# Attention with its quarters in pairs: another order of scores, raw tiles and weighted values on TensorE

## The chip, the cores and the metric

The kernel runs on one core of a Trainium2 chip. The metric is the device time of one execution in microseconds; the figure for a kernel is the median of several executions. Engines work in order, each through its own queue, and meet through semaphores: TensorE (PE, with its weight loads as PEld), VectorE (DVE), ScalarE (ACT), GpSimd (POOL) and SyncE (SP), which here only issues DMAs.

## What is computed

One block of a network on an input of 4 images of 32 x 32 tokens with 192 channels: a layer norm, attention with a decomposed relative position bias, a residual, a second layer norm, and a mixture of 8 experts of which each token takes one. Only the attention matters here:

```python
B, H, W, DIM, HEADS = (4, 32, 32, 192, 12)
HD = DIM // HEADS                       # 16
n = h * w                               # 1024 tokens
q, k, v = (qkv[0], qkv[1], qkv[2])      # (b * heads, n, hd)
rel_h = jnp.einsum('bhwc,hkc->bhwk', r_q, Rh)
rel_w = jnp.einsum('bhwc,wkc->bhwk', r_q, Rw)
bias = (rel_h[:, :, :, :, None] + rel_w[:, :, :, None, :]).reshape(b * heads, n, n)
attn = jax.nn.softmax(jnp.einsum('bnd,bmd->bnm', q * scale, k) + bias, axis=-1)
out = jnp.einsum('bnm,bmd->bnd', attn, v)
```

That is 4 x 12 = 48 maps of 1024 x 1024. The text calls each of the 48 a head and numbers them 0 to 47.

## The kernel before, in words

The stages run one after the other: projections with the relative terms (to about 138 us), the attention (to about 672 us), gate, routing and experts. Only the attention's function differs in the change.

**What a head needs.** The softmax subtracts a row maximum, which is found first. For a head, TensorE makes eight raw tiles (raw_scores, L750, matmuls at L759): 128 queries by 1024 keys, in one of two PSUM buffers (max_ps, two banks each). VectorE reduces each one to its negated maximum (take_max, L900, the reduce at L905). GpSimd repeats the maxima (L657), TensorE transposes them (transpose_max, L782, into a score bank), ScalarE copies them (copy_max, L865) and SyncE stores them as one more row of the queries' side (store_max). Only then are the scores proper made (scores, L787, matmul at L791): sixteen matmuls of 128 keys by 512 queries, k = 0 to 15, each into one of three PSUM banks (ring_ps). ScalarE takes the exponential of each (L888) into one of eight tiles of probs. weighted_values (L795, matmuls at L803) multiplies four of them with the values and adds into out_ps; a program line of eight matmuls there is sixteen in the trace, since the operands are four bytes wide. When all sixteen are in, ScalarE copies out_ps (copy_out, L872), TensorE turns it (turn_out, L809, matmuls at L812, into a score bank), and VectorE divides by the sums (normalize, L907 to L920, which ends with att_sb).

**The order.** A head is four quarters, u = 0 to 3. In each, TensorE issues scores 4u and 4u+1, a pair of raw tiles, scores 4u+2 and 4u+3, and weighted_values of the quarter before. The raw tiles are the last two of head n+1 in quarter 0, and the first six of head n+2 in quarters 1 to 3. Quarter 1 ends with transpose_max for head n+1, quarter 2 with turn_out for head n-1. VectorE's order is two reduces a quarter, and normalize of head n-1 behind those of quarter 2. ScalarE's is four exps a quarter, the output copy behind exp 3, and the copy of the maxima behind exp 7.

**The waits that the prediction uses.** A raw tile waits until the tile two before it is reduced (tile_max, L755), because its buffer is the same. The three score banks go around in turns; eighteen turns a head: sixteen scores, one turn for the transposed maxima (MAX_AT, turn 8) and one for the turned output (TURNED_AT, turn 13). bank_free (L763) finds what stood in the bank three turns before, and waits for its exp (exp_done), for the copy of the maxima (max_copied) or for normalize (att_done). With turn 13, the score at turn 16, k = 14, is the one that waits for att_done; scores 9 and 10 come at turns 10 and 11.

**Ends of the stage.** The heads run in groups of four; the first and the last group are written out, those between are a loop. Head 0 has no output of a head before; head 46 has raw tiles in quarter 0 alone and head 47 has none.

Of the kernel before, what the change touches and what calls it, by code (L numbers as in the profile page):

```python
# [552 lines left out]
def attention(nc, g):  # L553
# [7 lines left out]
    GROUP = 4  # L561
    RING = 2 * GROUP
    BANKS = 3
    MAX_AT, TURNED_AT, TURN = 8, 13, 2 * KT + 2
    HIGH = HD + 2 * HS
    with ExitStack() as ctx:
        sb = lambda name, shape, dt=F32: ctx.enter_context(nc.sbuf_tensor(name, shape, dt))
# [37 lines left out]
        def slot(s, ahead=0):  # L605

            return (s.slot + ahead) % SLOTS

        def head(s, ahead=0):


            return s.group + (s.slot + ahead) // SLOTS
# [132 lines left out]
        @block.tensor  # L745
        def _(pe):
            pe.wait_ge(consts_loaded, 16 * 2 * SLOTS)
            pe.wait_ge(ident_cast, 1)

            def raw_scores(n, j, t, reused):  # L750


                if reused:

                    pe.wait_ge(tile_max, KT * n + t - 1)  # L755
                for quarter in (0, 2, 1, 3):
                    at = quarter // 2 * LOWER
                    keys = slice(quarter * QN, (quarter + 1) * QN)
                    last = nc.tensor.matmul(max_ps[t % 2][:, keys], q_side[j][at:at + HIGH, quarter, t * P:(t + 1) * P],  # L759
                                            k_side[j][at:at + HIGH, keys], start=True, stop=True, skip_group_check=True, tile_position=(at, 0))  # L760
                last.then_inc(raw_ready, 1)

            def bank_free(s, at):  # L763

                at, back = at - BANKS, 0
                while True:
                    if at < 0:
                        at, back = at + TURN, 1  # L770
                        if not s.before(1):
                            return
                    if at == MAX_AT and (back or s.after(1)):
                        return pe.wait_ge(max_copied, s.n - back + 2)
                    if at == TURNED_AT and s.before(1 + back):
                        return pe.wait_ge(att_done, s.n - back)
                    if at not in (MAX_AT, TURNED_AT):
                        k = at - (at > MAX_AT) - (at > TURNED_AT)
                        return pe.wait_ge(exp_done, 2 * KT * (s.n - back) + k + 1)
                    at -= BANKS  # L780

            def transpose_max(n, j):  # L782
                pe.wait_ge(max_repeated, n + 1)
                nc.tensor.matmul(max_t_ps, max_copies[:, j % 2, :, :].rearrange("p q t -> p (q t)"), ident16[:],
                                 start=True, stop=True).then_inc(max_t_ready, 1)

            def scores(s, u, i):  # L787

                k, tile = GROUP * u + i, 2 * u + i // 2
                bank_free(s, turn_of(k))  # L790
                nc.tensor.matmul(ring_ps[turn_of(k) % BANKS][:], k_side[slot(s)][:, tile * P:(tile + 1) * P],  # L791
                                 q_side[slot(s)][:, tile // 2, (i % 2) * HALF:(i % 2 + 1) * HALF],
                                 start=True, stop=True).then_inc(scores_ready, 1)

            def weighted_values(n, j, u):  # L795


                pe.wait_ge(exp_done, 2 * KT * n + GROUP * u + GROUP)
                for i in range(2):
                    tile = 2 * u + i  # L800
                    for quarter in range(QUARTERS):
                        queries = slice(quarter % 2 * QN, (quarter % 2 + 1) * QN)
                        last = nc.tensor.matmul(out_ps[quarter * 2 * HD:(quarter + 1) * 2 * HD, :], values[j][:, tile, :],  # L803
                                                probs[:, u % 2 * GROUP + 2 * i + quarter // 2, queries],
                                                start=(tile == 0), stop=(tile == KT - 1), skip_group_check=True,
                                                tile_position=(0, quarter * 2 * HD))
                last.then_inc(group_done, 1)

            def turn_out(n):  # L809
                pe.wait_ge(out_copied, n + 1)  # L810
                for b in range(2):
                    last = nc.tensor.transpose(turned_ps[:, b * P:(b + 1) * P], out_t[:, b * P:(b + 1) * P], g.ident[:])  # L812
                last.then_inc(turned, 1)


            for n, tiles in ((0, KT), (1, 6)):
                pe.wait_ge(loaded[n], 16 * LOADS)
                for t in range(tiles):
                    raw_scores(n, n, t, KT * n + t >= 2)
                if n == 0:  # L820
                    transpose_max(0, 0)

            def step(s):
                for u in range(PAIR_TILES):
                    if u == 0:

                        pe.wait_ge(max_loaded[slot(s)], 16 * (head(s) + 1))
                    if u == 1 and s.after(2):
                        pe.wait_ge(loaded[slot(s, 2)], 16 * LOADS * (head(s, 2) + 1))
                    scores(s, u, 0)  # L830
                    scores(s, u, 1)
                    for i in range(2):

                        if u == 0 and s.after(1):
                            raw_scores(s.n + 1, slot(s, 1), 6 + i, True)
                        if u >= 1 and s.after(2):
                            raw_scores(s.n + 2, slot(s, 2), 2 * (u - 1) + i, True)
                    scores(s, u, 2)
                    scores(s, u, 3)
                    if u == 0 and s.before(1):  # L840
                        weighted_values(s.n - 1, slot(s, -1), PAIR_TILES - 1)
                    if u == 1:
                        pe.wait_ge(values_ready, s.n + 1)
                        if s.before(1):

                            pe.wait_ge(out_copied, s.n)
                    if u >= 1:
                        weighted_values(s.n, slot(s), u - 1)
                    if u == 1 and s.after(1):
                        bank_free(s, MAX_AT)  # L850
                        transpose_max(s.n + 1, slot(s, 1))
                    if u == 2 and s.before(1):
                        bank_free(s, TURNED_AT)
                        turn_out(s.n - 1)

            steps(pe, BH, SLOTS, step)
            weighted_values(BH - 1, (BH - 1) % SLOTS, PAIR_TILES - 1)
            pe.wait_ge(exp_done, 2 * KT * BH)
            turn_out(BH - 1)

        @block.scalar
        def _(act):
            nc.scalar.activation(ident16[:], g.ident[:], ACT.Copy).then_inc(ident_cast, 1)  # L863

            def copy_max(n, j, fills):  # L865
                act.wait_ge(max_t_ready, n + 1)
                if fills is not None:

                    act.wait_ge(max_loaded[(j - 2) % SLOTS], 16 * fills)
                nc.scalar.activation(max_rows[:, j % 2, :], max_t_ps, ACT.Copy).then_inc(max_copied, 1)  # L870

            def copy_out(n, reused):  # L872
                act.wait_ge(group_done, PAIR_TILES * (n + 1))
                if reused:
                    act.wait_ge(turned, n)
                nc.scalar.activation(out_t[:], out_ps[:], ACT.Copy).then_inc(out_copied, 1)

            copy_max(0, 0, None)

            def step(s):  # L880
                for u in range(PAIR_TILES):
                    for i in range(GROUP):
                        k = GROUP * u + i
                        if i == 0 and (s.before(1) or u >= 2):

                            act.wait_ge(group_done, PAIR_TILES * s.n + u - 1)
                        act.wait_ge(scores_ready, 2 * KT * s.n + k + 1)
                        nc.scalar.activation(probs[:, u % 2 * GROUP + i, :], ring_ps[turn_of(k) % BANKS][:], ACT.Exp).then_inc(exp_done, 1)  # L888
                        if u == 0 and i == 3 and s.before(1):
                            copy_out(s.n - 1, s.before(2))  # L890
                        if k + 1 == MAX_AT and s.after(1):

                            copy_max(s.n + 1, slot(s, 1), head(s, -1) + 1 if s.before(1) else None)

            steps(act, BH, SLOTS, step)
            copy_out(BH - 1, True)

# [787 lines left out]
```

## Time and profile before

| | us |
|---|---|
| median of three executions | 913.78 (912.25 to 915.0) |
| profiled execution | 914.5 |
| its span in the trace | 912.5 |
| attention, first to last output copy | 163.0 to 671.0 |
| PE, DVE, ACT busy over the span | 825.7, 726.4, 605.2 |

The profile is of one execution. PE counts as busy while a matmul is under way, and matmuls overlap; so a busy PE is not yet PE at its limit. Starts of neighbouring groups say more than their durations. In a timeline, a line is a run of like instructions: start, duration of the run, engine, line of the program, output and inputs, shapes, count. What stands in brackets is the idle time of the engine ahead of it, and who ended it.

### The profile page before, as it was taken

The numbers are of one execution on the slowest core, as the hardware profiler recorded it, in microseconds if no ns is written. First come the engines' busy times: TensorE is split into PE (matmuls) and PEld (weight loads), VectorE is DVE, ScalarE is ACT, GpSimd is POOL, SyncE is SP. The second block draws the span as 40 slices with busy tenths as digits, with TensorE's granted clock in tenths as the row PEclk, the third lists the DMA queues.
The fourth block names the chain that finished last, engine by engine and source line by source line (L and its number), as shares of the span: only waits on it lengthen the run. The fifth ranks groups of instructions, "written<-read, shape, count | busy, mean of one in ns | idle before, by whom it ended". The sixth has DMA issues, their size and how long they took to land. (4 is left out here: it accounts for less than half of the span.)

```text
span 912.5 us, 26072 instructions
## 1 busy us (share of the span) xinstructions
PE 825.7 (90%) x8906; PEld 465.2 (51%) x8906; DVE 726.4 (80%) x1019; ACT 605.2 (66%) x1140; POOL 274.8 (30%) x430
## 2 busy tenths in 40 slices
PE   3889937999999999999999999999979936999994
PEld 1657922333333333333333333333359926999994
DVE  6765867998989989999999989989527676888883
ACT  3555624888888888888888888888854403545452
POOL 3360000013343343302224342421114403555552
PEclk9899965999999999999999999999989757999997
DMA  6234883344554545444454444553034402222220
GB/s 170 78 102 123 347 287 93 99 120 130 141 132 116 128 131 140 116 115 131 116 139 133 131 130 134 143 141 102 7 146 138 156 24 61 84 84 78 89 61 11
DMA packets 69700, 109.60 MB, mean 120 GB/s; under 512 B 20107, under 2 KB 36649, under 8 KB 68114
## 3 DMA queue, kind: packets, MB, share of 16 engines
q1 hardware_dynamic: 59120, 75.49, 29.6%
q0 software_dynamic: 9216, 26.51, 10.0%
q10 hardware_dynamic: 1314, 6.95, 2.0%
q8 instruction: 30, 0.49, 0.2%
q14 instruction: 20, 0.16, 0.1%
HBM read 77.58 MB, written 33.19 MB: 121 GB/s over the span
## 5 line engine op out<-in xcount | busy, mean ns | idle before, releaser
L905 DVE TENSOR_REDUCE neg_max<-max_ps 128x1 f16<-128x1024 f32 x384 | 452.3, 1222 | 54.8 <-PE max_ps L759 54.4
L888 ACT ACTIVATE probs<-ring_ps 128x512 f32<-128x512 f32 x768 | 413.7, 595 | 69.7 <-PE ring_ps L791 68.3
L791 PE MATMUL ring_ps<-q_side,k_side 113*128 113x512 f16 x768 | 234.4, 387 | 6.5 <-DMA q_side<-rel_split 4.4
L803 PE MATMUL out_ps<-probs,values 128*32 128x256 f32 x3072 | 206.4, 386 | 0.1
L759 PE MATMUL max_ps<-k_side,q_side 48*128 48x256 f16 x1536 | 122.7, 279 | 16.0 <-ACT ident L863 9.6
L803 PEld LDWEIGHTS out_ps<-probs,values 128*32 128x32 f32 x3072 | 80.3, 109 | 111.1 <-ACT probs L888 56.5
L657 POOL COPY max_copies<-neg_max 128x32 f16<-128x32 f16 x48 | 10.1, 210 | 366.1 <-DVE neg_max L905 366.1
L759 PEld LDWEIGHTS max_ps<-k_side,q_side 48*128 48x128 f16 x1536 | 50.1, 95 | 114.7 <-issue 66.8
L791 PEld LDWEIGHTS ring_ps<-q_side,k_side 113*128 113x128 f16 x768 | 51.8, 97 | 105.4 <-ACT probs L888 74.1
L1438 PE MATMUL hid_ps<-slot_t,w_top 128*118 128x128 f16 x312 | 69.7, 223 | 0.8 <-ACT slot_t L1484 0.8
L1441 PE MATMUL hid_ps<-slot_t,w_tail 128*118 128x128 f16 x312 | 69.1, 221 | 0.0
L1440 PE MATMUL hid_ps<-slot_t,w_top 128*118 128x128 f16 x312 | 69.1, 221 | 0.0
L1439 PE MATMUL hid_ps<-slot_t,w_top 128*118 128x128 f16 x312 | 69.0, 221 | 0.0
L1442 PE MATMUL hid_ps<-slot_t,w_tail 128*118 128x128 f16 x312 | 69.0, 221 | 0.0
L1494 ACT ACTIVATE silu<-hid_ps 118x512 f32<-118x512 f32 x39 | 23.3, 597 | 50.1 <-PE hid_ps L1442 50.1
L1417 POOL DMA_INDIRECT out<-y,slot_token x39 | 39.6, 1014 | 54.8 <-issue 38.0
L1402 POOL DMA_INDIRECT slot_rows<-token_rows,slot_token x39 | 41.7, 1070 | 37.7 <-SPq L1365 26.1
L1541 DVE TENSOR_TENSOR hidden<-hid_ps,silu 118x512 f32<-118x512 f32 x39 | 27.0, 692 | 25.7 <-ACT silu L1494 18.2
L1438 PEld LDWEIGHTS hid_ps<-slot_t,w_top 128*118 128x118 f16 x312 | 42.0, 134 | 3.6 <-issue 1.3
L1442 PEld LDWEIGHTS hid_ps<-slot_t,w_tail 128*118 128x118 f16 x312 | 42.1, 135 | 0.0
L1439 PEld LDWEIGHTS hid_ps<-slot_t,w_top 128*118 128x118 f16 x312 | 42.1, 135 | 0.0
L1441 PEld LDWEIGHTS hid_ps<-slot_t,w_tail 128*118 128x118 f16 x312 | 42.1, 135 | 0.0
(216 smaller groups left out, 1339.2 us busy)
## 6 DMA issues: line engine op xcount, KB each, us to landing
q_side<-rel_split SPq DMA_DIRECT2D x384, 64.0 KB, 2.3
q_side<-qk_split SPq DMA_DIRECT2D x192, 64.0 KB, 2.5
rel_split<-expert_weights ACTq DMA_DIRECT2D x6, 1024.0 KB, 4.9
rel_split<-expert_weights SPq DMA_DIRECT2D x6, 1024.0 KB, 5.7
q_side<-qk_split SPq DMA_DIRECT2D x48, 128.0 KB, 2.8
k_side<-qk_split SPq DMA_DIRECT2D x144, 32.0 KB, 1.8
token_rows<-tn_parts SPq DMA_DIRECT2D x8, 512.0 KB, 2.9
expert_weights<-in_w_t POOLq DMA_DIRECT2D x32, 117.2 KB, 2.9
```

Source lines behind the costliest of these rows:

```text
L759: last = nc.tensor.matmul(max_ps[t % 2][:, keys], q_side[j][at:at + HIGH, quarter, t * P:(t + 1) * P], k_side[j][at:at + HIGH, keys], star ...
L791: nc.tensor.matmul(ring_ps[turn_of(k) % BANKS][:], k_side[slot(s)][:, tile * P:(tile + 1) * P], q_side[slot(s)][:, tile // 2, (i % 2) * HA ...
L803: last = nc.tensor.matmul(out_ps[quarter * 2 * HD:(quarter + 1) * 2 * HD, :], values[j][:, tile, :], probs[:, u % 2 * GROUP + 2 * i + quar ...
L888: nc.scalar.activation(probs[:, u % 2 * GROUP + i, :], ring_ps[turn_of(k) % BANKS][:], ACT.Exp).then_inc(exp_done, 1)
L905: nc.vector.tensor_reduce(neg_max[:, j % 2, t:t + 1], max_ps[t % 2][:], AX, ALU.max, negate=True).then_inc(tile_max, 1)
L1402: pool.indirect_dma_start(rows[:, j, :], None, g.token_rows, bass.IndirectOffsetOnAxis(ap=g.slot_token[:, n:n + 1], axis=0), bounds_check= ...
L1417: pool.indirect_dma_start(g.out_rows, bass.IndirectOffsetOnAxis(ap=g.slot_token[:, n:n + 1], axis=0), y[:, j, :], None, bounds_check=last_ ...
L1438: nc.tensor.matmul(out, w_top[:, j, h, 0, some], hi_top, start=True, stop=False, skip_group_check=True)
L1439: nc.tensor.matmul(out, w_top[:, j, h, 0, some], lo_top, start=False, stop=False, skip_group_check=True)
L1440: nc.tensor.matmul(out, w_top[:, j, h, 1, some], hi_top, start=False, stop=False, skip_group_check=True)
L1441: nc.tensor.matmul(out, w_tail[:, j, h, some], hi_tail, start=False, stop=False, skip_group_check=True)
L1442: last = nc.tensor.matmul(out, w_tail[:, j, h, some], lo_tail, start=False, stop=True, skip_group_check=True)
```

## The change

The four quarters are written as two pairs. In a pair (quarters u and u+1) TensorE now issues: scores 4u, 4u+1 and 4u+2; the raw pair of quarter u; weighted_values of the quarter before; three scores (4u+3, 4u+4, 4u+5); the raw pair of quarter u+1; scores 4u+6 and 4u+7; weighted_values of quarter u. turn_out moves from the end of quarter 2 to behind the weighted values in the middle, ahead of score 11, and with it the turn of its bank from 13 to 12. transpose_max stays behind the weighted values of quarter 0. On ScalarE the output copy goes ahead of exp 3 instead of behind it. The wait for the loads of head n+2 stands directly ahead of the raw pair of quarter 1. All counts stay the same.

```diff
-    MAX_AT, TURNED_AT, TURN = 8, 13, 2 * KT + 2
+    MAX_AT, TURNED_AT, TURN = 8, 12, 2 * KT + 2
...
             def step(s):
-                for u in range(PAIR_TILES):
+                pe.wait_ge(max_loaded[slot(s)], 16 * (head(s) + 1))
+                for u in range(0, PAIR_TILES, 2):
+                    for i in range(3):
+                        scores(s, u, i)
+                    raw_pair(s, u)
+                    if u:
+                        weighted_values(s.n, slot(s), u - 1)
+                    elif s.before(1):
+                        weighted_values(s.n - 1, slot(s, -1), PAIR_TILES - 1)
+                    if u and s.before(1):
+                        bank_free(s, TURNED_AT)
+                        turn_out(s.n - 1)
+                    scores(s, u, 3)
+                    scores(s, u + 1, 0)
+                    scores(s, u + 1, 1)
+                    if u == 0 and s.after(2):
+                        pe.wait_ge(loaded[slot(s, 2)], 16 * LOADS * (head(s, 2) + 1))
+                    raw_pair(s, u + 1)
+                    scores(s, u + 1, 2)
+                    scores(s, u + 1, 3)
...
+                    weighted_values(s.n, slot(s), u)
...
+                        if k == 3 and s.before(1):
+                            copy_out(s.n - 1, s.before(2))
                         act.wait_ge(scores_ready, 2 * KT * s.n + k + 1)
...
-                        if u == 0 and i == 3 and s.before(1):
-                            copy_out(s.n - 1, s.before(2))
```

raw_pair(s, u) issues the two raw tiles that belong to quarter u, as the loop did before.

TensorE in quarters 0 and 1 of head 2, before (q_side2 and k_side2 are this head's operands; max_ps0 and max_ps1 are the raw tiles, of heads 3 and then 4, whose operands lie in slot 0):

```order
L791 MATMUL ring_ps0<-q_side2,k_side2 128x512
L791 MATMUL ring_ps1<-q_side2,k_side2 128x512
L759 MATMUL max_ps0<-k_side3,q_side3 128x256 x4
L759 MATMUL max_ps1<-k_side3,q_side3 128x256 x4
L791 MATMUL ring_ps2<-q_side2,k_side2 128x512
L791 MATMUL ring_ps0<-q_side2,k_side2 128x512
L803 MATMUL out_ps<-probs,values1 32x256 x8
L791 MATMUL ring_ps1<-q_side2,k_side2 128x512
L791 MATMUL ring_ps2<-q_side2,k_side2 128x512
L759 MATMUL max_ps0<-k_side0,q_side0 128x256 x4
L759 MATMUL max_ps1<-k_side0,q_side0 128x256 x4
```

And of the change, the same place:

```order
L791 MATMUL ring_ps0<-q_side2,k_side2 128x512
L791 MATMUL ring_ps1<-q_side2,k_side2 128x512
L791 MATMUL ring_ps2<-q_side2,k_side2 128x512
L759 MATMUL max_ps0<-k_side3,q_side3 128x256 x4
L759 MATMUL max_ps1<-k_side3,q_side3 128x256 x4
L803 MATMUL out_ps<-probs,values1 32x256 x8
L791 MATMUL ring_ps0<-q_side2,k_side2 128x512
L791 MATMUL ring_ps1<-q_side2,k_side2 128x512
L791 MATMUL ring_ps2<-q_side2,k_side2 128x512
L759 MATMUL max_ps0<-k_side0,q_side0 128x256 x4
L759 MATMUL max_ps1<-k_side0,q_side0 128x256 x4
```

Between the two raw pairs there were two scores, the weighted values and two scores; now there are the weighted values and three scores.

TensorE in quarters 2 and 3 of head 2, before, from turn_out on, with the semaphores that each one waits for (raw tiles of head 4, in slot 0):

```order
L812 MATMUL ring_ps1<-ident_sb,out_t 128x128 [waits out_copied,exp_done]
L812 MATMUL ring_ps1<-ident_sb,out_t 128x128
L791 MATMUL ring_ps2<-q_side2,k_side2 128x512 [waits exp_done]
L791 MATMUL ring_ps0<-q_side2,k_side2 128x512 [waits exp_done]
L759 MATMUL max_ps0<-k_side0,q_side0 128x256 [waits tile_max]
L759 MATMUL max_ps0<-k_side0,q_side0 128x256 x3
L759 MATMUL max_ps1<-k_side0,q_side0 128x256 [waits tile_max]
L759 MATMUL max_ps1<-k_side0,q_side0 128x256 x3
L791 MATMUL ring_ps1<-q_side2,k_side2 128x512 [waits att_done]
L791 MATMUL ring_ps2<-q_side2,k_side2 128x512 [waits exp_done]
```

And of the change:

```order
L812 MATMUL ring_ps0<-ident_sb,out_t 128x128 [waits out_copied,exp_done]
L812 MATMUL ring_ps0<-ident_sb,out_t 128x128
L791 MATMUL ring_ps1<-q_side2,k_side2 128x512 [waits exp_done]
L791 MATMUL ring_ps2<-q_side2,k_side2 128x512 [waits exp_done]
L791 MATMUL ring_ps0<-q_side2,k_side2 128x512 [waits att_done]
L759 MATMUL max_ps0<-k_side0,q_side0 128x256 [waits tile_max]
L759 MATMUL max_ps0<-k_side0,q_side0 128x256 x3
L759 MATMUL max_ps1<-k_side0,q_side0 128x256 [waits tile_max]
L759 MATMUL max_ps1<-k_side0,q_side0 128x256 x3
L791 MATMUL ring_ps1<-q_side2,k_side2 128x512 [waits exp_done]
L791 MATMUL ring_ps2<-q_side2,k_side2 128x512 [waits exp_done]
```

The score that waits for att_done is now k = 13 and stands ahead of the raw pair of quarter 3; before it was k = 14, behind that pair.

## Rows read from the trace of the kernel before

**Rows 1.** Windows: length, busy PE, PEld, DVE, ACT, POOL, clock, DMA share, GB/s.
```profile
200.00:640.00 440.00, 437.36 (x4658) 163.00 (x4653) 397.08 (x407) 372.06 (x729) 132.42 (x235) 1.00 0.48 128
...
660.00:670.00 10.00, 8.78 (x85) 3.16 (x87) 0.50 (x2) 8.61 (x17) 0.00 (x0) 1.00 0.01 2
670.00:680.00 10.00, 5.88 (x40) 4.75 (x34) 2.38 (x5) 4.02 (x7) 2.34 (x1) 0.70 0.60 229
```

**Rows 2.** Timeline of TensorE's matmuls over one head in mid stage.
```profile
399.87 0.60 PE L791 MATMUL ring_ps<-q_side,k_side 113*128 113x512 f16 x2
400.40 0.62 PE L759 MATMUL max_ps<-k_side,q_side 48*128 48x256 f16 x8
...
401.50 1.07 PE L803 MATMUL out_ps<-probs,values 128*32 128x256 f32 x16
402.50 0.61 PE L791 MATMUL ring_ps<-q_side,k_side 113*128 113x512 f16 x2
403.04 0.61 PE L759 MATMUL max_ps<-k_side,q_side 48*128 48x256 f16 x8
403.58 0.60 PE L791 MATMUL ring_ps<-q_side,k_side 113*128 113x512 f16 x2
404.12 1.07 PE L803 MATMUL out_ps<-probs,values 128*32 128x256 f32 x16
405.00 0.22 PE L784 MATMUL ring_ps<-ident,max_copies 128*32 128x128 f16 x1
405.15 0.60 PE L791 MATMUL ring_ps<-q_side,k_side 113*128 113x512 f16 x2
405.69 0.61 PE L759 MATMUL max_ps<-k_side,q_side 48*128 48x256 f16 x8
...
406.77 1.07 PE L803 MATMUL out_ps<-probs,values 128*32 128x256 f32 x16
...
408.05 0.60 PE L791 MATMUL ring_ps<-q_side,k_side 113*128 113x512 f16 x2
408.58 0.61 PE L759 MATMUL max_ps<-k_side,q_side 48*128 48x256 f16 x8
409.12 0.61 PE L791 MATMUL ring_ps<-q_side,k_side 113*128 113x512 f16 x2
409.66 1.07 PE L803 MATMUL out_ps<-probs,values 128*32 128x256 f32 x16
410.66 0.39 PE L791 MATMUL ring_ps<-q_side,k_side 113*128 113x512 f16 x1
```

**Rows 3.** The line of the output copy: count, durations in ns, first and last start.
```profile
L876 ACT ACTIVATE out_t<-out_ps x48: 383/383/384, 163.0 to 671.0; 128x256 f32<-128x256 f32 x48
```

**Rows 4.** Timeline of VectorE over the same head.
```profile
403.47 2.36 DVE L905 TENSOR_REDUCE neg_max<-max_ps 128x1 f16<-128x1024 f32 x2 [0.27 <-PE max_ps L759]
406.13 2.36 DVE L905 TENSOR_REDUCE neg_max<-max_ps 128x1 f16<-128x1024 f32 x2 [0.30 <-PE max_ps L759]
...
408.74 0.29 DVE L920 TENSOR_TENSOR att_sb<-ring_ps,recip 128x128 f32 x1
```

**Rows 5.** TensorE's timeline from 403.5 on: the second raw tile of that pair.
```profile
403.27 0.38 PE L759 MATMUL max_ps<-k_side,q_side 48*128 48x256 f16 x4
```

**Rows 6.** Waits from 200 to 640 us: total, times, longest.
```profile
PEld ring_ps L791 <- DVE att_sb L920: 8.7, 41, 0.2
```

**Rows 7.** Timeline of ScalarE in the same head.
```profile
402.63 0.38 ACT L876 ACTIVATE out_t<-out_ps 128x256 f32<-128x256 f32 x1 [0.16 <-PE out_ps L803]
402.93 2.17 ACT L888 ACTIVATE probs<-ring_ps 128x512 f32<-128x512 f32 x4
405.29 0.27 ACT L870 ACTIVATE max_rows<-ring_ps 32x128 f16<-32x128 f32 x1 [0.20 <-PE ring_ps L784]
```

**Rows 8.** TensorE's timeline in head 0, where the granted clock was at its lower level.
```profile
149.90 1.03 PE L791 MATMUL ring_ps<-q_side,k_side 113*128 113x512 f16 x2 [1.91 <-DMA q_side<-rel_split]
150.87 1.03 PE L759 MATMUL max_ps<-k_side,q_side 48*128 48x256 f16 x8
```

## What I predicted before the changed kernel had run

> **What bounds the kernel now.** I read the windows of the attention stage first. From 200 to 640 us TensorE shows as busy in all but 2.6 of 440 us at full clock, while VectorE is busy for 397 us of it [rows 1]. "Busy" only says that matmuls overlap, so the next view is TensorE's timeline over one head (one of the 48 attention maps) [rows 2]. The starts give the price of each piece, gap to the next included. Two scores followed by raw tiles take 0.54 us (402.50 to 403.04); one more score in such a group adds 0.22 (0.61 less the 0.39 of one). The raw pair followed by scores takes 0.54, two scores followed by weighted values 0.54, weighted values followed by scores 1.00 (409.66 to 410.66), or 1.03 with the maxima's transpose behind them (404.12 to 405.15), or 1.28 with turn_out (406.77 to 408.05). A plain quarter is 0.54 + 0.54 + 0.54 + 1.00 = 2.62 and a head is 10.79 (399.87 to 410.66). Over all heads the output copies, 48 of them from 163.0 to 671.0, give 508 / 47 = 10.81 [rows 3].
>
> So far TensorE looks like the bound. VectorE's timeline tells the rest [rows 4]. The first raw tile of a pair at 403.04 lets its reduce start at 403.47 (0.43 later). The two reduces take 2.36 and end at 405.83. The second raw tile of a pair may not start before the second reduce of the pair before has emptied its PSUM buffer: those reduces began 0.44 behind the raw tiles of 400.40 (as 405.69 to 406.13) and ended at about 403.20, and the second raw tile starts at 403.27 [rows 5]. First raw tile to second raw tile of the next pair is therefore 403.27 - 400.40 = 2.87 us at least. In the order before, the natural distance is 2.62 + 0.23 = 2.85, so this **second loop, TensorE to VectorE and back, is as tight as TensorE's own order**. VectorE idles 0.27 to 0.30 a quarter, not because it has time but because both raw tiles of a pair come together.
>
> There is one more loop in each head. In quarter 2 turn_out writes the previous head's turned output into a score bank. normalize reads it, standing in VectorE's queue behind the two reduces of that quarter: it ends at 409.03 (408.74 + 0.29) [rows 4]. The score that reuses the bank is then the first behind raw pair 3, at 409.12. The waits show 41 of these, 8.7 us in all, 0.21 each [rows 6], the size of the gap that stands between pieces anyway. It is nearly free, because the raw pair of quarter 3 had gone out at 408.58, ahead of it.
>
> **The change part by part.** *Fewer switches on TensorE.* Two quarters had eight groups: four of scores (4 x 0.54), two raw, two of weighted values. Now there are seven: 0.76 + 0.76 + 0.54 = 2.06 for the scores instead of 2.16, so 0.10 less in two quarters. Raw tiles followed directly by weighted values do not occur in the trace. Bounds: nothing for the switch, so 0.46 for the two raw tiles (two steps of 0.23, 403.04 to 403.27), and at the dear end 0.46 + 0.28, the dearest insertion that the rows show (turn_out with its two matmuls, 1.28 less 1.00). I take 0.54, the nearest rows being raw to scores. Below it turns out not to matter.
>
> *Raw pairs at uneven distance.* Call the start of a raw pair zero. Inside a pair of quarters the order is raw, weighted values, three scores, raw: 0.54 + 1.00 + 0.76 = 2.30 to the next pair, and 2.53 to its second tile. It may not start before 2.87 [rows 5]. TensorE stands for 0.34 us in front of its own queue: two scores and weighted values are behind it. Between pairs of quarters the way is longer, and VectorE idles there. The unknown switch could cost 0.34 more or any amount less and the second tile would still come at 2.87.
>
> *The bank of turn_out moves from ring turn 13 to 12.* This is the expensive part. The turned output now lies in bank 0, and the score that comes three turns later is the thirteenth counted from zero. It stands **ahead of** raw pair 3, where in the old order the waiting score was behind it. Normalize is still queued behind the reduces of raw pair 2. TensorE would reach that score 0.54 + 1.28 + 0.44 = 2.26 after raw pair 2; it may go at 409.12 - 405.69 = 3.43 (raw pair 2 to the score that waits for normalize, as measured [rows 2, 4]). That is 1.17 us of stall. Behind it stand raw pair 3 and everything after; VectorE, done with normalize, has no raw tile and idles as well, so nothing is won back later.
>
> *The output copy on ScalarE goes ahead of exp 3.* It starts 1.13 behind the weighted values (401.50 to 402.63) [rows 2, 7], so 1.67 after raw pair 0, and frees ScalarE at 2.05; exp 3 would have begun at 0.54 + 1.00 + 0.43 = 1.97. It costs exp 3 0.08. With 0.54 an exp (2.17 for four) exp 7 ends at 4.77, while the copy of the maxima starts at 3.72 + 0.88 + 0.29 = 4.89 and ends at 5.16; score 10, which uses that bank, is due at 5.19. Margin nil: I give it 0 to 0.1 a head and take 0. The wait for loaded moves a few tenths of a microsecond later and costs nothing. SyncE's and GpSimd's orders don't change.
>
> *The sum.* The path that now closes one head: raw pair 2 to score 13, 3.43; score 13 to raw pair 3, 0.32; raw pair 3, 0.54; scores 14 and 15, 0.54; weighted values, 1.00; three scores of the next head, 0.76; raw pair 0 to second tile of raw pair 1, 2.87; that tile to score 6, 0.31 (403.27 to 403.58); scores 6 and 7, 0.54; weighted values with transpose, 1.03; scores 8 to 10, 0.76. Together **12.10 us against 10.79, 1.31 more a head**. It holds for heads 1 to 45, which have both raw pairs and a normalize: 45 x 1.31 = 59.0. Head 0 has no normalize, only uneven pairs, at low clock: 0 to 1, I take 0.5. Heads 46 and 47 have hardly any raw tiles: 0. Sum 59.5 on the profiled execution's own 914.5 us gives 974.0; the median before is 0.7 below that execution, so about **973 us**, 6.5% slower.
>
> **The rivals.** *A: the switches decide.* If neither loop held TensorE back, 0.10 less twice a head would be 48 x 0.2 = 9.6 us: 904. The Trainium skill (TensorEngine Tiling, Key Properties) says that changing the tiling mode drains the engine, and one drain fewer in eight is what this order has. The rows agree that a switch costs about 0.1 us, but a gain needs the raw tiles to find VectorE ready, and 2.87 against 2.53 speaks against it. It would need the second reduce to end over 0.3 us sooner. 4%.
>
> *B: normalize doesn't hold score 13,* and only the uneven pairs count. Then raw pair 2 to the second tile of pair 3 is 2.87 too; normalize (about 0.54) and two reduces then end at 5.70, so the next second tile comes at 5.77, and the half takes 5.77 - 0.23 = 5.54; the other half 2.87 + 0.31 + 0.54 + 1.03 + 0.76 = 5.51. 11.05 a head: 45 x 0.26 + 0.5 = 12 more, 926. Against it: VectorE works in order, and the old trace shows normalize ending just where the reduces let it. 6%.
>
> *C: the stalls bring TensorE's clock down.* TensorE would stand 1.5 of 12.1 us a head, the longest time 1.2. From 660 to 670 us it was idle for 1.2 of 10 us and kept 1.00; the clock fell only where it was idle for 4 of 10 (670 to 680) [rows 1]. At the low clock two scores before raw tiles take 0.97 instead of 0.54 [rows 8], 1.8 times; the 5.8 us of TensorE's own pieces on the path would grow by 4.6 a head. A quarter of the heads gives 11 x 4.6 = 51 more: 1024. The Trainium skill (TensorE: Matmul & The Clock Gate, "A second HAM failure mode: psum-queue depth-cycling") tells of a kernel whose short idles between groups made the clock swing; no row here shows that. 4%.
>
> **How the numbers follow.** The forecast's mechanism has 84%, A 4, B 6, C 4, something else 2. Within it: the path's eleven pieces are read to 0.01 and could be 0.1 short; the ScalarE margin adds up to 0.1 a head, a bank of the third score in a row as much: up to 9 us more, 983. Downwards the mean head may hide a part of the new stalls in its irregular waits (10.81 against 10.79 leaves little) and score 13 might come 0.2 sooner: 45 x 0.25 = 11 less, 962. The range is 962 to 984, leaving out the rivals. A measurement of this kernel can tell about 0.3% from no change. Faster by more has 4%, within it 1%, slower 95%.
>
> **What would show it.** Heads of about 12.1 us; a wait of scores for att_sb of 1.1 to 1.3 us once a head, about 55 us in all against 8.7 in the waits; a wait of the raw tiles for neg_max of about 0.5 once a head; VectorE idling before neg_max about 2 us a head; clock at 1.00. Wrong would be a head under 11.3 with no long wait for att_sb (A or B) or a clock below 1.00 (C).

## The result, and the profile after

The changed kernel took 967.2 us in the median (964.74 to 969.46) against 914.39 for the kernel before (912.25 to 915.24). The median before is now over four executions, where the table above had three. The ratio on record is 1.0589, with a 95% interval of 1.0556 to 1.0621; the two medians divided give 1.0578, inside it. The forecast was 973 with a range of 962 to 984. The profiled execution took 964.74, its span in the trace is 962.7.

TensorE's timeline over one head, as [rows 2] for the kernel before (start, duration of the run, engine, line, operation, names, shapes, count; in brackets the idle time ahead and who ended it):

```profile
406.97 0.61 PE L759 MATMUL max_ps<-k_side,q_side 48*128 48x256 f16 x8
407.51 1.07 PE L803 MATMUL out_ps<-probs,values 128*32 128x256 f32 x16
408.51 0.44 PE L812 MATMUL ring_ps<-ident_sb,out_t 128*128 128x128 f32 x2
408.78 0.60 PE L791 MATMUL ring_ps<-q_side,k_side 113*128 113x512 f16 x2
410.36 0.39 PE L791 MATMUL ring_ps<-q_side,k_side 113*128 113x512 f16 x1 [0.98 <-DVE att_sb L926]
410.68 0.61 PE L759 MATMUL max_ps<-k_side,q_side 48*128 48x256 f16 x8
411.23 0.61 PE L791 MATMUL ring_ps<-q_side,k_side 113*128 113x512 f16 x2
411.76 1.07 PE L803 MATMUL out_ps<-probs,values 128*32 128x256 f32 x16
412.76 0.82 PE L791 MATMUL ring_ps<-q_side,k_side 113*128 113x512 f16 x3
413.52 0.61 PE L759 MATMUL max_ps<-k_side,q_side 48*128 48x256 f16 x8
414.06 1.07 PE L803 MATMUL out_ps<-probs,values 128*32 128x256 f32 x16
415.06 0.82 PE L791 MATMUL ring_ps<-q_side,k_side 113*128 113x512 f16 x3
415.82 0.39 PE L759 MATMUL max_ps<-k_side,q_side 48*128 48x256 f16 x4
416.37 0.39 PE L759 MATMUL max_ps<-k_side,q_side 48*128 48x256 f16 x4 [0.16 <-DVE neg_max L911]
416.69 0.61 PE L791 MATMUL ring_ps<-q_side,k_side 113*128 113x512 f16 x2
417.23 1.07 PE L803 MATMUL out_ps<-probs,values 128*32 128x256 f32 x16
...
418.27 0.84 PE L791 MATMUL ring_ps<-q_side,k_side 113*128 113x512 f16 x3
419.04 0.61 PE L759 MATMUL max_ps<-k_side,q_side 48*128 48x256 f16 x8
```

From raw pair 2 to raw pair 2 is 419.04 - 406.97 = 12.07 us. Both stalls stand in it. Score 13 (410.36) comes 3.39 after raw pair 2, and raw pair 3 behind it. Scores 11 and 12 take 0.44 where a score follows them directly, so score 13 would have started at 408.78 + 0.44 = 409.22; it stands for 1.14. The raw pair at 415.82 is torn apart: its second tile is at 416.37, 0.55 later instead of 0.23, and 2.85 behind the pair of 413.52.

VectorE over the same stretch, as [rows 4]:

```profile
407.40 2.36 DVE L911 TENSOR_REDUCE neg_max<-max_ps 128x1 f16<-128x1024 f32 x2 [0.95 <-PE max_ps L759]
409.67 0.20 DVE L921 RECIPROCAL recip<-ring_ps 128x8 f32<-128x8 f32 x1
410.01 0.29 DVE L926 TENSOR_TENSOR att_sb<-ring_ps,recip 128x128 f32 x1
411.12 2.36 DVE L911 TENSOR_REDUCE neg_max<-max_ps 128x1 f16<-128x1024 f32 x2 [0.81 <-PE max_ps L759]
413.95 4.66 DVE L911 TENSOR_REDUCE neg_max<-max_ps 128x1 f16<-128x1024 f32 x4 [0.48 <-PE max_ps L759]
```

Normalize ends at 410.30 and score 13 starts 0.06 later. From there VectorE has nothing to reduce until 411.12. The four reduces from 413.95 on run without a gap: there TensorE waits for VectorE. In the three places in brackets VectorE waits for TensorE, 0.48 to 0.95 us at a time, where before it was 0.27 to 0.30.

The waits from 200 to 640 us (total, times, longest), as [rows 6]; the two queues of TensorE, weight loads and matmuls, record the same stall apart:

```profile
DVE neg_max L911 <- PE max_ps L759: 80.3, 109, 1.0
PEld ring_ps L791 <- DVE att_sb L926: 53.3, 36, 1.5
...
PE ring_ps L791 <- DVE att_sb L926: 35.6, 36, 1.0
PEld max_ps L759 <- DVE neg_max L911: 31.0, 72, 0.4
```

The wait for att_sb is 53.3 / 36 = 1.48 us a head on the weight loads, against 8.7 / 41 = 0.21 in [rows 6]. This record counts the usual 0.2 between groups and the loading ahead as well, so it is more than the stall of 1.14. The windows and the line of the output copy, as [rows 1, 3]:

```profile
200.00:640.00 440.00, 398.34 (x4171) 153.84 (x4169) 354.29 (x363) 330.00 (x653) 123.25 (x216) 1.00 0.41 116
```

```profile
L882 ACT ACTIVATE out_t<-out_ps x48: 384/384/402, 160.9 to 724.4; 128x256 f32<-128x256 f32 x48
```

TensorE is idle for 41.7 of 440 us and its clock stays at 1.00. First to last output copy takes 563.5 us against 508.0.

### The profile page after: what moved, and what is told of

It is laid out like the page before. It is cut to its first block and busy times, and to the rows that moved or that the text cites. A ratio compares the mean times of both kernels' runs of the same rounds, so it can differ in the third digit from the quotient of the medians.

```text
span 962.7 us, 26072 instructions
## 1 busy us (share of the span) xinstructions
PE 828.8 (86%) x8906; PEld 470.4 (49%) x8906; DVE 723.2 (75%) x1019; ACT 601.2 (62%) x1140; POOL 276.1 (29%) x430
## 5 line engine op out<-in xcount | busy, mean ns | idle before, releaser
L791 PE MATMUL ring_ps<-q_side,k_side 113*128 113x512 f16 x768 | 228.6, 386 | 45.3 <-DVE att_sb L926 44.3
L759 PE MATMUL max_ps<-k_side,q_side 48*128 48x256 f16 x1536 | 129.9, 279 | 23.6 <-DVE neg_max L911 13.4
L791 PEld LDWEIGHTS ring_ps<-q_side,k_side 113*128 113x128 f16 x768 | 55.8, 97 | 173.5 <-DVE att_sb L926 67.3
L803 PEld LDWEIGHTS out_ps<-probs,values 128*32 128x32 f32 x3072 | 80.3, 109 | 94.7 <-ACT probs L896 30.8
L759 PEld LDWEIGHTS max_ps<-k_side,q_side 48*128 48x128 f16 x1536 | 55.7, 95 | 106.8 <-DVE neg_max L911 51.4
L1444 PEld LDWEIGHTS hid_ps<-slot_t,w_top 128*118 128x118 f16 x312 | 41.8, 134 | 4.1 <-issue 1.8
L1445 PEld LDWEIGHTS hid_ps<-slot_t,w_top 128*118 128x118 f16 x312 | 42.0, 134 | 0.0
L1446 PEld LDWEIGHTS hid_ps<-slot_t,w_top 128*118 128x118 f16 x312 | 42.0, 134 | 0.0
L1447 PEld LDWEIGHTS hid_ps<-slot_t,w_tail 128*118 128x118 f16 x312 | 41.9, 134 | 0.0
```

What stands on the lines that cost most here:

```text
L1444: nc.tensor.matmul(out, w_top[:, j, h, 0, some], hi_top, start=True, stop=False, skip_group_check=True)
L1445: nc.tensor.matmul(out, w_top[:, j, h, 0, some], lo_top, start=False, stop=False, skip_group_check=True)
L1446: nc.tensor.matmul(out, w_top[:, j, h, 1, some], hi_top, start=False, stop=False, skip_group_check=True)
L1447: nc.tensor.matmul(out, w_tail[:, j, h, some], hi_tail, start=False, stop=False, skip_group_check=True)
```

## The experiments

Each kernel ran beside the kernel before on the same chip; ratios are to that kernel's time there (median 912.13 us for the first four, 912.45 for the three with half reduces). "A head" is the mean distance of output copies over the first 44 of the 47 intervals, the ends of the stage left out. For the kernel before it is 10.87 us, for the changed one 12.11. The kernel before has eight long intervals, 10.93 to 11.73, which raise its mean; its middle interval (the median of the 44) is 10.80.

**The bank of turn_out moved back.** The changed order, with turn_out one score later:

```diff
-    MAX_AT, TURNED_AT, TURN = 8, 12, 2 * KT + 2
+    MAX_AT, TURNED_AT, TURN = 8, 13, 2 * KT + 2
...
+                    scores(s, u, 3)
                     if u and s.before(1):
                         bank_free(s, TURNED_AT)
                         turn_out(s.n - 1)
-                    scores(s, u, 3)
```

> The changed kernel with one thing undone: turn_out goes behind score 11 instead of ahead of it, its bank gets turn 13 again, so that score 14, behind raw pair 3, is the one that waits for normalize. Theory (normalize holds score 13 ahead of raw pair 3): the wait of scores for att_sb falls from 1.5 to about 0.2 us a head. Not all of it comes back: score 13 now uses score 11's bank and waits for its exp (turn_out between them), about 0.4. Head 11.2 us, time about 930 (924 to 938). If instead the time of the change comes from the uneven raw pairs, or from the new order as such, the kernel stays at 955 or more.

Measured: 930.39 us, ratio 1.0211 (1.0171 to 1.0251), 11.34 a head. TensorE in quarters 2 and 3:

```profile
404.46 0.61 PE L759 MATMUL max_ps<-k_side,q_side 48*128 48x256 f16 x8
405.00 1.07 PE L803 MATMUL out_ps<-probs,values 128*32 128x256 f32 x16
406.00 0.39 PE L791 MATMUL ring_ps<-q_side,k_side 113*128 113x512 f16 x1
406.23 0.38 PE L812 MATMUL ring_ps<-ident_sb,out_t 128*128 128x128 f32 x2
406.45 0.38 PE L791 MATMUL ring_ps<-q_side,k_side 113*128 113x512 f16 x1
407.08 0.39 PE L791 MATMUL ring_ps<-q_side,k_side 113*128 113x512 f16 x1 [0.25 <-ACT probs L896]
407.40 0.61 PE L759 MATMUL max_ps<-k_side,q_side 48*128 48x256 f16 x8
```

Raw pair 2 to raw pair 3 is 2.94 us instead of 3.71. Moving turn_out one score later, its bank with it, is worth 0.77 us a head. The wait for att_sb falls to 0.21 a head, as expected:

```profile
PEld ring_ps L791 <- DVE att_sb L926: 8.2, 39, 0.2
```

Not all comes back: score 13 now waits for the exp of score 11, as expected, and starts 0.63 behind score 12 instead of 0.22.

**The same bank in the old order.** The kernel before, with turn_out between scores 10 and 11:

```diff
-    MAX_AT, TURNED_AT, TURN = 8, 13, 2 * KT + 2
+    MAX_AT, TURNED_AT, TURN = 8, 12, 2 * KT + 2
...
                     scores(s, u, 2)
+                    if u == 2 and s.before(1):
+                        bank_free(s, TURNED_AT)
+                        turn_out(s.n - 1)
                     scores(s, u, 3)
...
-                    if u == 2 and s.before(1):
-                        bank_free(s, TURNED_AT)
-                        turn_out(s.n - 1)
```

> The order of the kernel before, with only turn_out moved: between scores 10 and 11, bank at turn 12. Raw pairs stay evenly spaced. Score 13, ahead of raw pair 3, waits for normalize. Theory: that wait alone makes the head 11.6 us (raw pair 2 to score 13 is 3.43 as before, raw pair 3 follows 0.32 later, 3.75 instead of 2.88), time about 948 (940 to 956). Rival (the pairs' uneven distance is the cost, the bank is not): within 5 us of 914.

Measured: 945.68 us, ratio 1.0381 (1.0347 to 1.0415), 11.62 a head. The raw pairs stand evenly in the issue order here, and the kernel still loses nearly two thirds of what the change loses. TensorE, from the score ahead of the waiting one:

```profile
401.46 0.39 PE L791 MATMUL ring_ps<-q_side,k_side 113*128 113x512 f16 x1
402.51 0.39 PE L791 MATMUL ring_ps<-q_side,k_side 113*128 113x512 f16 x1 [0.65 <-DVE att_sb L920]
402.83 0.61 PE L759 MATMUL max_ps<-k_side,q_side 48*128 48x256 f16 x8
```

So the order of the groups isn't needed for this part. That a score waits for normalize ahead of raw pair 3 is enough.

**The new order in quarters 0 and 1 only.** The loop over pairs of quarters runs for u = 0; quarters 2 and 3 and the bank of turn_out are as before; ScalarE's order is the changed one:

```diff
-    MAX_AT, TURNED_AT, TURN = 8, 12, 2 * KT + 2
+    MAX_AT, TURNED_AT, TURN = 8, 13, 2 * KT + 2
...
+                for u in range(2, PAIR_TILES):
+                    scores(s, u, 0)
+                    scores(s, u, 1)
+                    raw_pair(s, u)
+                    scores(s, u, 2)
+                    scores(s, u, 3)
+                    weighted_values(s.n, slot(s), u - 1)
+                    if u == 2 and s.before(1):
+                        bank_free(s, TURNED_AT)
+                        turn_out(s.n - 1)
```

> Quarters 0 and 1 in the new order (with the new place of the output copy on ScalarE), quarters 2 and 3 and turn_out with its bank at turn 13 in the old one. This leaves the uneven raw pairs and one switch fewer. Theory: the second tile of raw pair 1 waits 0.3 to 0.4 us a head for neg_max; the head is 10.95 to 11.05 us, the first head shorter by 2 as in the change; time 916 to 924. Rival A (a saved switch is a gain): 910 or less.

Measured: 917.32 us, ratio 1.0063 (1.0042 to 1.0084), 11.01 a head, 0.14 more than the mean before and 0.21 more than its middle interval. The torn pair shows:

```profile
404.20 0.82 PE L791 MATMUL ring_ps<-q_side,k_side 113*128 113x512 f16 x3
404.95 0.39 PE L759 MATMUL max_ps<-k_side,q_side 48*128 48x256 f16 x4
405.50 0.39 PE L759 MATMUL max_ps<-k_side,q_side 48*128 48x256 f16 x4 [0.16 <-DVE neg_max L913]
```

The uneven distance costs, but little: the smaller of the two mechanisms. The second tile stands for 0.32 (405.50 less 404.95 less 0.23), the saved switch gives 0.10 back, and 0.22 is left, which is the 0.21 of the middle interval.

The two costs taken alone don't add up to the change: 0.75 and 0.14 are 0.89 of 1.25 a head. The rest shows in the timelines. In the kernel before, the raw pairs start at 405.69, 408.58 and, a quarter on, at

```profile
411.20 0.62 PE L759 MATMUL max_ps<-k_side,q_side 48*128 48x256 f16 x8
```

Raw pair 2 to raw pair 3 grows from 2.89 to 3.71, raw pair 3 to the next raw pair 0 from 2.62 to 2.84, and from there to the next raw pair 2 from 5.29 (400.40 to 405.69) to 5.52. In the new order one score fewer and one switch fewer stand ahead of score 13. TensorE arrives there sooner and only waits longer, 1.14 us against 0.83 in the old order (402.51 less 401.46 less 0.22), while the score that moved takes its time behind raw pair 3.

**The output copy back behind exp 3.** The changed kernel with ScalarE's old order:

```diff
-                        if k == 3 and s.before(1):
-                            copy_out(s.n - 1, s.before(2))
...
+                        if k == 3 and s.before(1):
+                            copy_out(s.n - 1, s.before(2))
```

> The changed kernel with the output copy on ScalarE back behind exp 3. Exp 3 cannot start before score 3, which now stands behind the weighted values, so the copy, ready before that, comes 0.4 to 0.9 later and with it exps 4 to 7 and the copy of the maxima. Theory: that is 0.2 us a head on the path through scores 6 to 10, time 976 (970 to 982). Rival (ScalarE has slack everywhere): unchanged at 967.

Measured: 965.39 us, ratio 1.0595 (1.0565 to 1.0625), the interval of the change itself, and 12.11 a head, the same. My expectation was wrong. ScalarE in this kernel:

```profile
402.52 0.60 ACT L894 ACTIVATE probs<-ring_ps 128x512 f32<-128x512 f32 x1 [0.72 <-PE ring_ps L791]
403.02 0.38 ACT L882 ACTIVATE out_t<-out_ps 128x256 f32<-128x256 f32 x1
403.28 2.08 ACT L894 ACTIVATE probs<-ring_ps 128x512 f32<-128x512 f32 x4
405.52 0.27 ACT L876 ACTIVATE max_rows<-ring_ps 32x128 f16<-32x128 f32 x1 [0.16 <-PE ring_ps L784]
```

and in the changed kernel:

```profile
403.04 0.38 ACT L882 ACTIVATE out_t<-out_ps 128x256 f32<-128x256 f32 x1 [0.43 <-PE out_ps L803]
403.33 2.71 ACT L896 ACTIVATE probs<-ring_ps 128x512 f32<-128x512 f32 x5
406.32 0.27 ACT L876 ACTIVATE max_rows<-ring_ps 32x128 f16<-32x128 f32 x1 [0.28 <-PE ring_ps L784]
```

Counted from score 3 (402.10 here, 402.90 there), the output copy starts 0.78 later (0.92 instead of 0.14), but exp 3 starts 0.42 behind the score here and 0.43 there: the copy ahead of it only fills a time in which ScalarE waits for score 3. Exp 7 ends at 3.26 instead of 3.14, so 0.12 later and not 0.4 to 0.9. The copy of the maxima waits for its transpose in both of these heads; from 200 to 640 us this wait is recorded 37 times in the changed kernel and 18 times here, so the margin is used up in about half of the heads. The place of this copy costs nothing that the time shows.

**Half reduces.** In three kernels each reduce reads 512 of the 1024 keys, so that the maximum over the other half is left out; this shortens VectorE's two reduces from 2.36 to 1.29 us and changes nothing in any order:

```diff
-                nc.vector.tensor_reduce(neg_max[:, j % 2, t:t + 1], max_ps[t % 2][:], AX, ALU.max, negate=True).then_inc(tile_max, 1)
+                nc.vector.tensor_reduce(neg_max[:, j % 2, t:t + 1], max_ps[t % 2][:, 0:HALF], AX, ALU.max, negate=True).then_inc(tile_max, 1)
```

On the kernel before:

> The kernel before, but each reduce reads 512 of its 1024 keys (the maximum over the other half is left out), so that VectorE's part of the loop falls from 2.36 to about 1.3 us a pair. Theory: TensorE's own order was nearly as tight as the loop, so little comes back: 10.6 a head instead of 10.8, 0.2 x 47 = 9 us less, about 903 to 908. If VectorE had been the bound, 40 us or more would come back.

Measured: 906.68 us, ratio 0.9941 (0.9920 to 0.9962), 10.79 a head. VectorE loses over 45% of its reduce time and the kernel 0.6%. TensorE's own order was the other bound, hardly looser. The time fell where I expected it, the head didn't: I had written 10.6. The middle interval hardly moved, 10.78 against 10.80; most of the 0.08 is that seven of the eight long intervals are gone.

On the changed kernel:

> The changed kernel with the same half reduces. Theory: both VectorE's parts of the loss shrink, the second raw tile of raw pair 1 no longer waits, and the wait of score 13 for normalize falls to the time from turn_out on, about 0.5 us instead of 1.3; 11.1 a head, about 1.0 less than the changed kernel: 920 to 930. Rival (the new order itself costs TensorE its time, whatever VectorE does): 955 or more.

Measured: 924.06 us, ratio 1.0116 (1.0089 to 1.0144), 11.19 a head. Of the change's 5.9% only 1.2% is left, or 1.9% above the half-reduce kernel in the old order. The wait for normalize is still there, shorter (0.30 us of idle time on the matmuls instead of 0.98), and now it comes from turn_out and no longer from the reduces: VectorE itself waits for the turned output.

```profile
402.34 0.39 PE L791 MATMUL ring_ps<-q_side,k_side 113*128 113x512 f16 x1 [0.30 <-DVE att_sb L926]
```

```profile
400.05 1.29 DVE L911 TENSOR_REDUCE neg_max<-max_ps 128x1 f16<-128x512 f32 x2 [1.66 <-PE max_ps L759]
401.64 0.21 DVE L921 RECIPROCAL recip<-ring_ps 128x8 f32<-128x8 f32 x1 [0.29 <-PE ring_ps L812]
```

On the kernel with the new order in quarters 0 and 1 only:

> New order in quarters 0 and 1 only, old order and turn 13 in quarters 2 and 3, with half reduces. Nothing of VectorE is in the way now, so the saved switch (0.1 us a head, 5 us) should show against x5_old_half_reduce if rival A's arithmetic holds on TensorE. My working says that ScalarE takes it back: exp 3 waits behind the output copy, scores 7 and 9 then wait 0.1 each for their banks' exps, 10.66 against 10.58 a head. Expected: 0 to 4 us above x5; rival A: 4 to 6 below it.

Measured: 900.94 us, ratio 0.9876 (0.9851 to 0.9901), 10.74 a head. That is 5.7 us below the old order with half reduces, with intervals that don't touch, and rival A's arithmetic rather than mine. With full reduces the same order lost 0.6%. Whether a group less pays thus depends on VectorE. This kernel also has ScalarE's new order and the later wait for the loads, which no run takes apart here. The timeline doesn't settle why it pays so much: the second raw tile no longer waits, but scores 6 and 7 take 0.65 us (409.32 to 409.97) in the head below and 0.58 in the one before it, instead of 0.54, because score 7 waits for an exp as my working had it. That eats the saved 0.1 wholly or in part. The means of the two profiled executions differ by 0.05 a head, 2 us in all, less than the medians do: the profiled execution of the old order with half reduces (903.23) is the fastest of its seven, 3.5 us under their median, so its trace can't show most of the difference.

```profile
408.78 0.61 PE L759 MATMUL max_ps<-k_side,q_side 48*128 48x256 f16 x8
409.32 0.72 PE L791 MATMUL ring_ps<-q_side,k_side 113*128 113x512 f16 x2
409.97 1.07 PE L803 MATMUL out_ps<-probs,values 128*32 128x256 f32 x16
```

## Why the prediction was right, point by point

**The path.** All eleven pieces can be checked in the timeline above. Raw pair 2 to score 13 is 3.39 (forecast 3.43), then 0.32, 0.55, 0.53, 1.00, 0.76, then 2.85 (2.87) to the second tile of raw pair 1, then 0.32, 0.54, 1.04, 0.77. That makes 12.07 against 12.10. The move of the bank was the main term; it is shown twice: undone in the new order (0.77 us a head back) and done alone in the old one (0.75 more a head). That the stall is VectorE's work is shown a third way: with half reduces the same change costs 0.40 a head (11.19 against 10.79) and not 1.25.

**The signs.** VectorE idles before neg_max for 80.3 us in 440, 2.2 a head, where I had written about 2. The waits for att_sb come to 53.3 us against my 55, and there the closeness is luck: I had 1.1 to 1.3 each, which fits the stall of 1.14 (forecast 1.17), but the record that I took it from has 1.48 each, and its window holds 36 of the heads and not 45.

**The unknown switch.** Raw tiles followed by weighted values take 0.54 (406.97 to 407.51), the value taken. It isn't on the path, since both ways that it lies on end in a wait.

**The uneven pairs.** The stall before the second tile was to be 0.34 and is 0.32 (416.37 - 415.82 less 0.23). Its net price is smaller than that, 0.21 a head against a plain head before, because one switch of 0.10 is saved; against the mean before it is 0.14.

**The ScalarE terms.** Taken as nothing, and the experiment found nothing. Three scores in a row ahead of raw pair 2 took 0.77 to 0.86 in the heads read instead of 0.76; the 0.1 that I had allowed for occurs, but not in every head.

**Where 6 us of the forecast went.** The median came out 6 us under 973. The profiled execution, for which the sum was made, came out 9.3 us under 974.0, and there each part can be read. Between the profiled executions the span grew by 50.2 us, where the sum said 59.5. Interval by interval of the output copies: the first 44 grew by 54.8 (12.11 against 10.87), so 1.25 each and not 1.31. The step that was mis-sized is the old head: I took the 10.79 of one head, while 10.87 is the mean over these 44. Eight of them are 10.93 to 11.73 us long. From 200 to 640 us scores wait for a load six times there, 2.5 us in all. In the changed kernel no interval is over 12.17 and no such wait is recorded. Two things can have covered them, the stalls and the later place of the wait for the loads. Either may be enough: the profiled execution of the old order with turn 12, which has one stall and the old place of the wait, shows no such wait, and that of the new order in quarters 0 and 1 only, with the later place and the small stall, shows 0.6 us of them. I had looked at the mean over all 47 intervals, 10.81, which holds the two short last ones and so hid this. The steady heads come to about 3 us. The last three intervals grew by 0.7 together, where I had one full head (1.31): 0.6 us.

The second miss is head 0. I gave it 0.5 more, and the first output copy comes 2.1 us earlier: 2.6 us. In the kernel before, the wait for the loads of head 2 stood ahead of scores 4 and 5; now it is behind three scores.

The wait was 1.91 us, until 149.90 [rows 8]; in the changed kernel, at the same place of TensorE's timeline:

```profile
148.96 1.03 PE L759 MATMUL max_ps<-k_side,q_side 48*128 48x256 f16 x8 [0.37 <-DMA q_side<-rel_split]
```

I had written that this move costs nothing, which is right, and not seen that it gains where the load is late. The gain is no accident of one execution. From the first raw tiles of head 1 to the raw pair of quarter 1 of head 0 it is 12.05 us in the kernel before and 11.99 in the old order with turn 12, against 10.06 in the changed kernel and 9.98 to 10.24 in the three other kernels with the new quarters 0 and 1 and full reduces. About half of it is that the load itself lands sooner, 10.0 to 10.2 us after those first raw tiles instead of 11.0 to 11.1, in the same kernels. Why it does, no run shows.

The stages behind the attention took 3.2 us less (238.3 against 241.5 from the last output copy on) with no change in them. In the nine profiled executions here this part takes 235.4 to 241.5, without regard to the order in the attention, so this part of the miss is scatter. The four parts, 3, 0.6, 2.6 and 3.2, make up the 9.3 within rounding.

**The rivals.** A fell: the kernel got slower. Its 0.10 a switch isn't refuted, and in quarters 0 and 1 alone it is what turns a stall of 0.32 into a cost of 0.21. But the two stalls of a head, 1.14 and 0.32, take more than its two switches give. B fell: score 13 waited. C fell: TensorE was idle for 9.5% of the stage, in pieces of up to 1 us, and the granted clock stayed at 1.00.

## What to carry to other kernels

When an operation on the critical engine moves, look at which buffer it now takes, who reuses that buffer, and what stands behind the one who waits: the same wait was free behind the work that feeds the other engine, and cost 0.75 us a head ahead of it. Where two engines feed each other through two buffers, measure the distance from one pair to the next against the loop's own time (2.87 us here): moving time from one gap to the other gains nothing on the long side and stalls on the short one. For a price per round, take the mean over the steady rounds and not one clean round, since a new stall also swallows the small irregular waits.

## What I had not expected

With half reduces, the kernel with one group less a head was 5.7 us faster than the one without, where I expected 0 to 4 slower; the traces don't show where most of that comes from. And the output copy on ScalarE, 0.38 us in front of four exps that TensorE needs, can stand on either side of exp 3 without any effect: 12.11 a head both ways.
